# Destination one-hots compared in 16 bits by VectorE and spread to fp32 by ScalarE

## The chip, the cores and the metric

The kernel runs on one core of a Trainium2 chip. Its time is the device time of that core, in microseconds, from runs of the whole program. One core has five engines that each run their own list of instructions in order: TensorE (PE; its weight loads are shown as PEld), VectorE (DVE), ScalarE (ACT), GpSimd (POOL) and SyncE (SP), whose list here only issues DMAs. They wait for each other through semaphores.

## The reference

Four graph layers on 3125 nodes with 128 features and 103,125 edges sorted by destination, each followed by a residual and a layer norm. What matters here is the third layer's sum of edge attributes (64 features) per destination, and the number of edges per node, which the other layers use:

```python
agg = jax.ops.segment_sum(edge_attr, col, num_segments=x.shape[0])
h = jnp.concatenate([x, agg, u[batch]], axis=1)
...
x = _layernorm(x + _L0_gnn_ref(x, W1, b1, W2, b2, edge_index), axis=-1)
x = _layernorm(x + _L1_gnn_ref(x, src, dst, ...), axis=-1)
x = _layernorm(x + _L2_gnn_ref(x, edge_index, edge_attr_64, u, batch0, ...), axis=-1)
x = _layernorm(x + _L3_gnn_ref(x, src, dst, ...), axis=-1)
```

## The kernel before

The first 222 us build two things from the edge list; the rest (the four layers proper) multiplies node features with a matrix of edge counts and is not touched by the change.

**The loop.** It runs over 32 groups g. A group holds 20 blocks of 5 destinations, for which the counts between sources and destinations are made, and 4 edge blocks of 25 destinations (`EB` = 4, `EW` = 25), for which the attributes are summed. The last group has a quarter of both. No scheduler sets the order: each engine's list is written out, and semaphores tie them.

- VectorE makes three one-hots per group: `oh_lo` (L1119, 5000 elements of bf16) and `oh_key` (L1124, 4000 elements), both laid in pairs of 16-bit values and used for the counts, and `oh_dst` (L1157): for every edge slot of the 4 edge blocks, 32 per partition (`TE` = 8 each), 25 values that say which destination it has. `oh_dst` is fp32 and lies in `rowb`; it is made from int32 destinations `dst_e` with one scalar_tensor_tensor (add, then is_equal with `iota_w`). In the first groups VectorE also makes lists of edges (`make_lists`), and in group 5 some checks.
- TensorE waits for `oh_lo` and `oh_key` of a group, makes its 5 units of 4 blocks (L1740, L1744) in 5 banks, then waits for `dst_hot` and for the attributes (`ea_ready`) and makes the attribute products: per edge block 8 fp32 products with `oh_dst` as weights (L1756) and 8 with the upper halves of the same fp32 one-hots, read as bf16, for the number of edges (L1760). Then it folds the sums of the group before (`fold_quads`, L1701), and in groups 17 to 30 it does one step for x (transposes, L1715, or x times W, L1725).
- ScalarE copies each unit from its bank to `counts` (L802, five per group), keeps the attribute sums (`keep_apart`, L769, after the products of this group), keeps the folded ones (`keep_edges`, L775, after the fold of the group before), issues two of the loads of destinations (`odd_list`, L761), and in groups 17 to 30 keeps the x step (L783 or L789). In the first groups it also keeps lists (`keep_lists`, L746, L748).
- SP issues one attribute load of 256 KB per edge block (L583), up to 8 blocks ahead, each after the products of the block 8 before; for every second block a load of destinations (L575); and along blocks 36 to 60 the loads of x (L589).

Semaphores of this part: `dst_ready` (destinations landed), `dst_hot` (`oh_dst` made), `ea_made` (an edge block's products done), `apart_kept`, `apart_made` and `ea_kept` (the three steps behind it), `unit_made` and `unit_kept`.

Of the kernel before, what the change touches and what calls it, by code (L numbers as in the profile page):

```python
# [46 lines left out]
EW = 25  # L47
# [29 lines left out]
def gnn_program(nc, x, src, dst, edge_attr, p, out):  # L77

    with ExitStack() as ctx:
# [91 lines left out]
        def carve(n):  # L171
# [3 lines left out]
        iota_l = carve(128).bitcast(BF16).rearrange("p (l j) -> p l j", j=2)  # L175
        iota_w = wl1[:, 400:400 + EB * TE * EW].rearrange("p (j w) -> p j w", w=EW)
        dst_e = carve(RD * TE).bitcast(I32).rearrange("p (r j) -> p r j", r=RD)
        starts_i = carve(NE + 1)[0:1, :].bitcast(I32)
        key_base = carve(NQ)
# [64 lines left out]
            "bias_split ea_twice fold_made fold_kept masks_made l2_b1 l2_b2 bu_made flag_part flag_made "  # L244
            "deg_turned xw_made xw_kept apart_made apart_kept g_table_made g_key_made g_hot g_used g_kept o_table_made o_key_made o_hot o_used o_kept deg_again g_idx_seen before_made before_summed next_in sqrt_made"
        ).split()}
# [400 lines left out]
        def _(pool):  # L647
# [6 lines left out]
            for m in (ident, ident_bf, ident_h):  # L654
# [8 lines left out]
                           allow_small_or_imprecise_dtypes=True)  # L663
            nc.gpsimd.iota(iota_w, pattern=[[EW, EB], [0, TE], [1, EW]], base=0, channel_multiplier=0,
                           allow_small_or_imprecise_dtypes=True)
            for a, n in ((0, NQ - 1), (NQ - 1, 1)):
# [48 lines left out]
        def _(act):  # L715
# [40 lines left out]
            def odd_list(e):  # L756
# [4 lines left out]
                act.dma_start(dst_e[:, e % RD, :], dst[bass.ds(first, ECAP)].rearrange("(p j) -> p j", j=TE)).then_inc(dst_ready[e // EB % 3], 16)  # L761

            def keep_apart(g):

                ne = len(edge_blocks(g))
                act.wait_ge(s["ea_made"], EB * g + ne)
                if g >= 2:
                    act.wait_ge(s["apart_made"], g - 1)
                nc.scalar.activation(apart[:, g % 2, 0:ne, :], bank[5 + g % 2][:, 0:ne * (DE + 1)].rearrange("p (k f) -> p k f", k=ne), ACT.Copy).then_inc(s["apart_kept"], 1)  # L769
# [22 lines left out]
            for e in range(1, RD, 2):  # L792
                odd_list(e)
            keep_lists(0)
            act.wait_ge(s["pad_made"], 1)
            for g in range(NGP):
                for u, (ug, i, n) in enumerate(UNITS):
                    if ug != g:
                        continue
                    act.wait_ge(s["unit_made"], u + 1)  # L800
                    d0 = (g * GB + i) * BW
                    nc.scalar.activation(counts[:, :, d0:d0 + n * BW],  # L802
                                         bank[u % UB][:LO, 0:n * BK].rearrange("p (d h) -> p h d", h=HI), ACT.Copy).then_inc(s["unit_kept"], 1)
                if 1 <= g + 1 < NQ:
                    keep_lists(g + 1)
# [220 lines left out]
        def _(dve):  # L1026
# [86 lines left out]
            for g in range(NGP):  # L1113
# [38 lines left out]
                ne = len(es)  # L1152
                dve.wait_ge(dst_ready[g % 3], 16 * sum(len(edge_blocks(i)) for i in range(g % 3, g + 1, 3)))
                if g >= 2:
                    dve.wait_ge(s["ea_made"], EB * (g - 1))
                r0 = es[0] % RD
                nc.vector.scalar_tensor_tensor(oh_dst[r][:, 0:ne * TE, :],  # L1157
                                               dst_e[:, r0:r0 + ne, :].rearrange("p e (j a) -> p (e j) a", a=1).to_broadcast([128, ne * TE, EW]), -float(EB * g * EW),
                                               iota_w[:, 0:ne * TE, :],
                                               ALU.add, ALU.is_equal).then_inc(s["dst_hot"], 1)  # L1160

# [975 lines left out]
```

## Time and profile before

| | us |
|---|---|
| median of 3 runs | 818.76 (818.02 to 819.24) |
| the profiled execution | 820.66 |
| its span, first to last instruction | 818.6 |
| busy in the span: TensorE | 716.1 |
| VectorE | 585.3 |
| ScalarE | 330.6 |
| the loop over the groups | 26 to 222 |

The page gives for each engine its busy time in the span; these are averages over stages with different limits, so the loop has to be read by itself, through busy times of stretches, the order in time of one engine, and the chain of waits. The profiled execution is a single one, 1.9 us longer than the median; 2.1 us of it lie outside the span. Instructions of one engine overlap a little: the next may start before the last has ended, so what an instruction costs its queue is the distance from start to start.

### The profile page before, as it was taken

To read this page: it belongs to the slowest core of one execution; us is meant where nothing else is said; L and a number is where in the kernel's file an instruction comes from. 1 tells how busy PE (TensorE), PEld (TensorE's weight loads), DVE (VectorE), ACT (ScalarE), POOL (GpSimd) and SP (SyncE) were. 2 spreads that over 40 slices of the span, in tenths; PEclk is the share of its full clock that TensorE was granted. 3 is DMA by queue.
4 is the path that set the end of the run, shared out by engine and by line. 5 is a ranking of instruction groups with operands and counts; after the bars stand their busy time and mean duration, and the time that the engine had idled before them with its cause. 6 is when DMAs were issued, how large, how long until landed. Compare 5 with 4: busy or idle time off the path is not lost.

```text
span 818.6 us, 18498 instructions
## 1 busy us (share of the span) xinstructions
PE 716.1 (87%) x7630; PEld 640.1 (78%) x7630; DVE 585.3 (71%) x885; ACT 330.6 (40%) x594; POOL 25.5 (3%) x44
## 2 busy tenths in 40 slices
PE   4476776888889998999989998779969999999994
PEld 2366766888889998899979995445549998799994
DVE  6999999999776678778777764667576454145554
ACT  0365554666653224322462232363333332332243
POOL 4700000000000000000000000000000000000000
PEclk9777989999879999999999999989989999999998
DMA  4455677767530000000000000000000000000001
GB/s 104 136 136 160 180 213 204 190 186 211 143 84 1 1 1 1 1 1 1 2 22 1 1 1 2 0 14 0 1 26 1 0 0 1 1 1 1 1 26 54
DMA packets 48320, 43.14 MB, mean 53 GB/s; under 512 B 25989, under 2 KB 30759, under 8 KB 48167
## 3 DMA queue, kind: packets, MB, share of 16 engines
q1 hardware_dynamic: 35660, 39.80, 17.3%
q10 hardware_dynamic: 11932, 0.81, 1.0%
q8 instruction: 63, 1.03, 0.5%
q0 software_dynamic: 640, 1.29, 0.5%
q14 instruction: 25, 0.20, 0.1%
HBM read 39.08 MB, written 2.00 MB: 50 GB/s over the span
## 4 chain that ended last, share of the span: by engine, by line
PE 66%; DVE 16%; SPq 8%; issue 4%; ACT 2%; DMA 2%; DVEq 0%; ACTq 0%
PE bank L1823 21%; PE bank L1824 21%; SPq L583 3%; SPq L575 3%; PE bank L2024 2%; SPq L580 2%; DVE early L1119 2%; PE bank L1740 2%; PE bank L1756 2%; PE bank L2032 2%; PE bank L1885 1%; DVE early L1124 1%; PE bank L2075 1%; PE bank L2076 1%; PE bank L1744 1%
## 5 line engine op out<-in xcount | busy, mean ns | idle before, releaser
L1823 PE MATMUL bank<-stage,f_hi 125*128 125x392 f32 x1000 | 348.6, 349 | 2.5 <-issue 2.3
L1824 PE MATMUL bank<-stage,f_lo 125*128 125x392 f32 x1000 | 342.3, 342 | 0.0
L1202 DVE CAST stage<-counts 125x2352 fp32r<-125x2352 uint8 x120 | 164.4, 1380 | 80.8 <-PE bank L1824 80.7
L846 ACT ACTIVATE stage<-counts 125x1568 fp32r<-125x1568 uint8 x80 | 108.1, 1351 | 227.2 <-PE bank L1824 224.8
L1823 PEld LDWEIGHTS bank<-stage,f_hi 125*128 125x128 f32 x1000 | 189.8, 190 | 4.1 <-issue 2.4
L1824 PEld LDWEIGHTS bank<-stage,f_lo 125*128 125x128 f32 x1000 | 189.7, 190 | 0.6
L1740 PE MATMUL bank<-early 128*128 128x125 bf16 x625 | 76.8, 241 | 31.3 <-issue 24.0
L802 ACT ACTIVATE counts<-bank 125x500 uint8<-125x500 f32 (+1 forms) x157 | 81.2, 595 | 43.0 <-PE bank L1744 39.8
L1740 PEld LDWEIGHTS bank<-early 128*128 128x128 bf16 x625 | 68.2, 111 | 33.6 <-issue 33.6
L1119 DVE TENSOR_TENSOR early<-tmp 128x5000 bf16<-128x5000 bf16 (+1 forms) x32 | 86.4, 2700 | 1.4 <-PE bank L1744 1.4
L1744 PE MATMUL bank<-early 128*128 128x75 bf16 x625 | 76.2, 218 | 2.3 <-issue 2.1
L1124 DVE TENSOR_TENSOR early<-tmp,early 128x4000 bf16<-128x4000 bf16 (+1 forms) x32 | 70.2, 2193 | 0.0
L1744 PEld LDWEIGHTS bank<-early 128*128 128x128 bf16 x625 | 67.4, 109 | 2.4 <-issue 2.3
L1357 DVE SCALAR_TENSOR_TENSOR tmp<-bank,counts 125x2000 uint8<-125x2000 uint8 (+7 forms) x32 | 45.5, 1423 | 1.4
L1756 PE MATMUL bank<-wb,rowb 128*32 128x64 f32 x1520 | 36.2, 239 | 11.4 <-DMA wb<-in_edge_attr 6.0
L1756 PEld LDWEIGHTS bank<-wb,rowb 128*32 128x32 f32 x1520 | 29.3, 120 | 15.6 <-issue 13.3
L1157 DVE SCALAR_TENSOR_TENSOR rowb<-tmp,wl 128x800 f32<-128x800 int32 (+1 forms) x32 | 31.1, 971 | 0.1
L1885 PEld LDWEIGHTS bank<-ident,wa 128*125 128x125 f32 x100 | 17.8, 234 | 16.6 <-issue 7.2
L1760 PE MATMUL bank<-wb,rowb 128*32 128x1 bf16 x1000 | 28.8, 168 | 0.8 <-issue 0.8
L1885 PE MATMUL bank<-ident,wa 128*125 128x128 f32 x100 | 19.4, 321 | 11.1 <-ACT wb L878 6.4
L1280 DVE TENSOR_TENSOR f_lo<-bank,f_hi 125x512 fp32r<-125x512 f32 (+1 forms) x14 | 8.4, 631 | 26.7 <-ACT f_hi L860 26.7
L1249 DVE TENSOR_TENSOR wa<-bank,rowb 128x392 f32<-128x392 f32 x16 | 9.1, 567 | 24.0 <-PE bank L1824 23.8
(248 smaller groups left out, 848.1 us busy)
## 6 DMA issues: line engine op xcount, KB each, us to landing
wb<-in_edge_attr SPq DMA_DIRECT2D x95, 256.0 KB, 3.2
rowb<-in_edge_attr SPq DMA_DIRECT2D x30, 256.0 KB, 3.3
wa<-in_x SPq DMA_DIRECT2D x12, 125.0 KB
out<-wl SPq DMA_DIRECT2D x6, 250.0 KB
tmp<-in_dst SPq DMA_DIRECT2D x63, 4.0 KB, 2.9
tmp<-in_dst ACTq DMA_DIRECT2D x62, 4.0 KB, 2.8
eaT<-eaT SPq DMA_DIRECT2D x1, 784.0 KB, 6.0
wb<-in_L_gnn_w_ih SPq DMA_DIRECT2D x1, 384.0 KB, 3.4
```

The lines of the kernel that those rows point to most:

```text
L802: nc.scalar.activation(counts[:, :, d0:d0 + n * BW], bank[u % UB][:LO, 0:n * BK].rearrange("p (d h) -> p h d", h=HI), ACT.Copy).then_inc(s ...
L846: nc.scalar.activation(set_buffer(u, m), counts[:, SETS[u][0]:sum(SETS[u]), chunk(c)], ACT.Copy).then_inc(s["set_a_ready"], 1)
L1119: nc.vector.tensor_tensor(oh_lo[r][:, 0:n, 0:LO, :], iota_l.rearrange("p (a l) j -> p a l j", a=1)[:, :, 0:LO, :].to_broadcast([128, n, LO ...
L1124: hot = nc.vector.tensor_tensor(oh_key[r][:, 0:half, :, :, :].rearrange("p b m k j -> p (b m) k j"), iota_l.rearrange("p (a l) j -> p a l ...
L1202: nc.vector.tensor_copy(set_buffer(u, m), counts[:, SETS[u][0]:sum(SETS[u]), chunk(pair * 2 + off)]).then_inc(s["set_d_ready"], 1)
L1357: nc.vector.scalar_tensor_tensor(junk.rearrange("p (g l q) -> p g l q", g=n, q=2), turned, 0.0, own, ALU.add, ALU.not_equal, accum_out=unl ...
L1740: mm(bank[u % UB][:, b * BK:(b + 1) * BK], oh_lo[r][:, i + b, :, 0], keys[:, 0:BK], start=True, stop=False)
L1744: last = mm(bank[u % UB][:, b * BK + 2 * HI:(b + 1) * BK], oh_lo[r][:, i + b, :, 1], keys[:, BK:NK * HI], start=False, stop=True)
L1756: mm(bank[5 + r][quad:quad + 32, k * (DE + 1):k * (DE + 1) + DE], oh_dst_row[r][:, at:at + 32], ea_in[e % RE][:, j, :], start=(j < 4), sto ...
L1823: mm(bank[h][:, 0:CH], f_hi[:, first + k, :], rhs[:, k, :], start=(first + k == 0), stop=False)
L1824: last = mm(bank[h][:, 0:CH], f_lo[:, first + k, :], rhs[:, k, :], start=False, stop=(first + k == HI - 1))
L1885: last = nc.tensor.transpose(bank[NORM_BANK[i][k]][:LO, h * D:(h + 1) * D], norm_columns(i, k, h), ident[:, :])
```

## The change

Where `oh_dst` was made by one instruction of VectorE in 32 bits, it is now made in three steps. ScalarE shortens the destinations of a group to bf16, minus the group's first destination (`shorten`, 32 elements per partition, one group ahead, behind the units of the group before). VectorE compares them in 16 bits in pairs (tensor_tensor, is_equal, 800 elements) with numbers that `iota_l` already holds, into `oh_short`. ScalarE spreads these bf16 one-hots to fp32 in their old place (`spread_bits`), behind the second of the five unit copies of the same group. Two semaphores are new: `dst_short` and `dst_bits`. `dst_hot` now comes from ScalarE. `iota_w` and its iota on GpSimd are gone.

```diff
-        iota_w = wl1[:, 400:400 + EB * TE * EW].rearrange("p (j w) -> p j w", w=EW)
+        oh_short = [wl1[:, 400 + r * nh // 2:400 + (r + 1) * nh // 2].bitcast(BF16).rearrange("p (j w t) -> p j w t", w=EW, t=2) for r in range(2)]
+        dst_short = carve(EB * TE).bitcast(BF16).rearrange("p (r j t) -> p r j t", r=2, t=2)
...
-            nc.gpsimd.iota(iota_w, pattern=[[EW, EB], [0, TE], [1, EW]], base=0, channel_multiplier=0,
-                           allow_small_or_imprecise_dtypes=True)
...
+            def shorten(g):
+
+                es = edge_blocks(g)
+                act.wait_ge(dst_ready[g % 3], 16 * sum(len(edge_blocks(i)) for i in range(g % 3, g + 1, 3)))
+                if g >= 2:
+                    act.wait_ge(s["dst_bits"], g - 1)
+                n, r0 = len(es), es[0] % RD
+                nc.scalar.activation(dst_short[:, g % 2, 0:n * TE // 2, :].rearrange("p j t -> p (j t)"), dst_e[:, r0:r0 + n, :].rearrange("p r j -> p (r j)"),
+                                     ACT.Copy, bias=-float(EB * g * EW)).then_inc(s["dst_short"], 1)
+
+            def spread_bits(g):
+
+                n = len(edge_blocks(g)) * TE
+                act.wait_ge(s["dst_bits"], g + 1)
+                if g >= 2:
+                    act.wait_ge(s["ea_made"], EB * (g - 1))
+                nc.scalar.activation(oh_dst[g % 2][:, 0:n, :].rearrange("p (j t) w -> p j t w", t=2), oh_short[g % 2][:, 0:n // 2, :, :].rearrange("p j w t -> p j t w"),
+                                     ACT.Copy).then_inc(s["dst_hot"], 1)
...
             keep_lists(0)
+            shorten(0)
...
                                          bank[u % UB][:LO, 0:n * BK].rearrange("p (d h) -> p h d", h=HI), ACT.Copy).then_inc(s["unit_kept"], 1)
+                    if i == 4:
+                        spread_bits(g)
+                if g + 1 < NGP:
+                    shorten(g + 1)
...
-                dve.wait_ge(dst_ready[g % 3], 16 * sum(len(edge_blocks(i)) for i in range(g % 3, g + 1, 3)))
+                dve.wait_ge(s["dst_short"], g + 1)
                 if g >= 2:
-                    dve.wait_ge(s["ea_made"], EB * (g - 1))
-                r0 = es[0] % RD
-                nc.vector.scalar_tensor_tensor(oh_dst[r][:, 0:ne * TE, :],
-                                               dst_e[:, r0:r0 + ne, :].rearrange("p e (j a) -> p (e j) a", a=1).to_broadcast([128, ne * TE, EW]), -float(EB * g * EW),
-                                               iota_w[:, 0:ne * TE, :],
-                                               ALU.add, ALU.is_equal).then_inc(s["dst_hot"], 1)
+                    dve.wait_ge(s["dst_hot"], g - 1)
+                shape = [128, ne, TE // 2, EW, 2]
+                half = ne * TE // 2
+                nc.vector.tensor_tensor(oh_short[r][:, 0:half, :, :].rearrange("p (k j) w t -> p k j w t", k=ne),
+                                        iota_l[:, 0:ne * EW, :].rearrange("p (k a w) t -> p k a w t", k=ne, a=1).to_broadcast(shape),
+                                        dst_short[:, r, 0:half, :].rearrange("p (k j) (a t) -> p k j a t", k=ne, a=1).to_broadcast(shape),
+                                        ALU.is_equal).then_inc(s["dst_bits"], 1)
```

On ScalarE, in a group with an x step (such as 27), this stood before: the five unit copies (L802), the two keeps, two list loads and the keep of an x step. `counts`, `wl` (the sums), `eaT` (the folded ones) and `xT` are what is written; `bank` is PSUM.

```order
L802 ACTIVATE counts<-bank 125x25x20 [waits unit_made] x5
L769 ACTIVATE wl<-bank 128x260 [waits apart_made,ea_made]
L775 ACTIVATE eaT<-bank 65x100 [waits apart_made]
L760 TENSOR_LOAD tmp
L761 REGISTER_ALU
L761 DMA tmp<-in_dst 128x8
L760 TENSOR_LOAD tmp
L761 REGISTER_ALU
L761 DMA tmp<-in_dst 128x8
L783 ACTIVATE xT<-bank 128x500 [waits xt_made]
```

And this stands there now, up to the keep of the x step, which follows as before (line numbers are those of the changed kernel):

```order
L821 ACTIVATE counts<-bank 125x25x20 [waits unit_made] x2
L778 ACTIVATE rowb<-wl 128x800 [waits ea_made,dst_bits]
L821 ACTIVATE counts<-bank 125x25x20 [waits unit_made] x3
L769 ACTIVATE tmp<-tmp 128x32 [waits dst_bits,dst_ready0]
L787 ACTIVATE wl<-bank 128x260 [waits apart_made,ea_made]
L793 ACTIVATE eaT<-bank 65x100 [waits apart_made]
L759 TENSOR_LOAD tmp
L760 REGISTER_ALU
L760 DMA tmp<-in_dst 128x8
L759 TENSOR_LOAD tmp
L760 REGISTER_ALU
L760 DMA tmp<-in_dst 128x8
```

The spread (L778) has come behind the second copy, and the shortening (L769) between the last copy and the keeps; nothing else moved.

On VectorE a group of three instructions, and the two after it, before:

```order
L1119 TENSOR_TENSOR early<-tmp 128x20x250 [waits unit_made,list_kept]
L1124 TENSOR_TENSOR early<-tmp,early 128x4000
L1157 SCALAR_TENSOR_TENSOR rowb<-tmp,wl 128x800 [waits ea_made,dst_ready1]
L1119 TENSOR_TENSOR early<-tmp 128x20x250 [waits unit_made,list_kept]
L1124 TENSOR_TENSOR early<-tmp,early 128x4000
```

And now:

```order
L1142 TENSOR_TENSOR early<-tmp 128x20x250 [waits unit_made,list_kept]
L1147 TENSOR_TENSOR early<-tmp,early 128x4000
L1181 TENSOR_TENSOR wl<-tmp 128x800 [waits dst_hot,dst_short]
L1142 TENSOR_TENSOR early<-tmp 128x20x250 [waits unit_made,list_kept]
L1147 TENSOR_TENSOR early<-tmp,early 128x4000
```

The compare keeps its place; it waits for two semaphores of ScalarE instead of a DMA and TensorE, and writes `wl` (where `oh_short` lies) instead of `rowb`.

## Rows read from the trace of the kernel before

**Rows 1.** Busy us (instructions) of each engine in two stretches; granted clock, DMA share, GB/s.

```profile
core 0: us, PE busy (x) PEld busy (x) DVE busy (x) ACT busy (x) POOL busy (x), PEclk, DMA share, GB/s
...
95.00:133.00 38.00, 28.07 (x894) 26.68 (x895) 38.00 (x21) 19.26 (x43) 0.00 (x0) 0.91 0.72 203
...
148.00:222.00 74.00, 66.42 (x2101) 62.96 (x2098) 70.74 (x40) 49.42 (x113) 0.00 (x0) 0.95 0.69 185
```

**Rows 2.** Order in time, VectorE, one group: start us, duration us, instruction.

```profile
199.34 0.99 DVE L1157 SCALAR_TENSOR_TENSOR rowb<-tmp,wl 128x800 f32<-128x800 int32 x1
200.24 2.76 DVE L1119 TENSOR_TENSOR early<-tmp 128x5000 bf16<-128x5000 bf16 x1
202.91 2.24 DVE L1124 TENSOR_TENSOR early<-tmp,early 128x4000 bf16<-128x4000 bf16 x1
205.07 0.99 DVE L1157 SCALAR_TENSOR_TENSOR rowb<-tmp,wl 128x800 f32<-128x800 int32 x1
```

**Rows 3.** The chain of waits, 176 to 200 us, shares by line.

```profile
by line: SPq L583 23.4%; SPq L575 21.7%; SPq L580 14.6%; issue 12.8%; DMA wb<-in_edge_attr 12.6%; PE bank L1756 5.6%; PE bank L1725 4.2%; PE bank L1701 2.4%; PE bank L1740 1.6%; PE bank L1760 0.8%; PE bank L1744 0.5%
```

**Rows 4.** Order in time, SP's queue: x loads, then block 72, then block 121.

```profile
124.46 0.36 SPq L589 DMA_DIRECT2D wa<-in_x  x1
...
127.55 0.35 SPq L589 DMA_DIRECT2D wa<-in_x  x1
...
143.29 0.63 SPq L583 DMA_DIRECT2D wb<-in_edge_attr  x1
...
212.03 3.04 SPq L583 DMA_DIRECT2D wb<-in_edge_attr  x4
```

**Rows 5.** Order in time, ScalarE: first copies of groups 17 and 28.

```profile
146.96 2.50 ACT L802 ACTIVATE counts<-bank 125x500 uint8<-125x500 f32 x5 [1.41 <-PE bank L1744]
...
206.41 2.98 ACT L802 ACTIVATE counts<-bank 125x500 uint8<-125x500 f32 x5 [0.49 <-PE bank L1744]
```

**Rows 6.** Order in time, ScalarE: a group with hardly a wait.

```profile
185.13 2.50 ACT L802 ACTIVATE counts<-bank 125x500 uint8<-125x500 f32 x5
187.47 0.44 ACT L769 ACTIVATE wl<-bank 128x260 f32<-128x260 f32 x1
...
189.87 2.50 ACT L802 ACTIVATE counts<-bank 125x500 uint8<-125x500 f32 x5
```

**Rows 7.** Order in time, VectorE: a small 16-bit compare and its successor.

```profile
218.83 0.32 DVE L1129 TENSOR_TENSOR tmp<-tmp,wl 128x300 bf16<-128x300 bf16 x1
219.06 0.37 DVE L1157 SCALAR_TENSOR_TENSOR rowb<-tmp,wl 128x200 f32<-128x200 int32 x1
```

**Rows 8.** Groups of ScalarE's instructions by shape: busy us, mean ns, idle before.

```profile
L846 ACT ACTIVATE stage<-counts 125x1176 fp32r<-125x1176 uint8 x40 | 47.5, 1187 | 149.5 <-PE bank L1824 149.5
...
L825 ACT ACTIVATE f_hi<-wa 125x512 fp32r<-125x512 f32 x6 | 3.2, 627 | 0.0
...
L746 ACT ACTIVATE tmp<-bank 128x252 bf16<-128x252 bf16 x5 | 1.9, 377 | 12.7 <-PE bank L1693 12.7
```

**Rows 9.** Order in time, all engines: group 27's steps, and group 28's products.

```profile
200.42 2.50 ACT L802 ACTIVATE counts<-bank 125x500 uint8<-125x500 f32 x5
...
201.77 0.43 PE L1756 MATMUL bank<-wb,rowb 128*32 128x64 f32 x16
...
203.17 0.39 ACT L769 ACTIVATE wl<-bank 128x260 f32<-128x260 f32 x1 [0.25 <-PE bank L1760]
...
203.69 0.25 ACT L775 ACTIVATE eaT<-bank 65x100 f32<-65x100 f32 x1
...
205.34 0.59 ACT L783 ACTIVATE xT<-bank 128x500 f32<-128x500 f32 x1 [1.40 <-issue]
...
208.70 0.65 PE L1756 MATMUL bank<-wb,rowb 128*32 128x64 f32 x16
...
211.21 0.25 ACT L775 ACTIVATE eaT<-bank 65x100 f32<-65x100 f32 x1
```

**Rows 10.** Order in time, ScalarE and its DMA issues (ACTq).

```profile
155.19 0.34 ACTq L761 DMA_DIRECT2D tmp<-in_dst  x1
155.55 0.45 ACT L769 ACTIVATE wl<-bank 128x260 f32<-128x260 f32 x1
```

More of the change, by code:

```diff
@@ L244, in gnn_program @@
             "bias_split ea_twice fold_made fold_kept masks_made l2_b1 l2_b2 bu_made flag_part flag_made "
-            "deg_turned xw_made xw_kept apart_made apart_kept g_table_made g_key_made g_hot g_used g_kept o_table_made o_key_made o_hot o_used o_kept deg_again g_idx_seen before_made before_summed next_in sqrt_made"
+            "deg_turned xw_made xw_kept apart_made apart_kept g_table_made g_key_made g_hot g_used g_kept o_table_made o_key_made o_hot o_used o_kept deg_again g_idx_seen before_made before_summed next_in sqrt_made dst_short dst_bits"
         ).split()}
```

## The prediction

> **What bounds the kernel now.** The change touches only the loop over the 32 groups, 26 to 222 us, so I took the busy times of two stretches of it: in 38 us VectorE works 38.0, TensorE 28.1, ScalarE 19.3; in the last 74 us they work 70.7, 66.4 and 49.4 [rows 1]. VectorE is full. Its order in time says why: one group is three instructions, starting at 199.34, 200.24 and 202.91, and the next group's first starts at 205.07. A group takes 5.73 us, of which the compare of destinations (L1157) holds 0.90 [rows 2].
>
> That is not yet the bound of the loop's end. The chain of waits from 176 to 200 us lies on SP's queue, 23.4, 21.7 and 14.6% in its three lines, then on the landing of a load [rows 3]. SP issues two attribute loads and one list of destinations per two edge blocks. Block 72 was issued at 143.29 and block 121 at 212.03: 68.7 us for 49 blocks, 5.6 us per group of four. Between 88 and 130 us it also issues the 13 loads of x, and then two blocks take 3.1 us (124.46 to 127.55), 6.2 us per group [rows 4]. So three things lie close together: VectorE 5.73, SP 5.6, and 6.2 in groups 9 to 15, where the products run late behind the loads. Later the kernel catches up: ScalarE begins group 17 at 146.96 and group 28 at 206.41, 11 groups in 59.45 us, 5.40 each [rows 5].
>
> **ScalarE's cycle before.** In a group that waits for almost nothing ScalarE starts five copies at 185.13, the keep of the sums at 187.47 (2.34 later) and the next group's copies at 189.87: 4.74 us, one step of x included [rows 6]. That is 1 us below VectorE's cycle. This room is what lets the loop catch up.
>
> **The change, part by part.** (1) *VectorE's compare.* The old one, 800 elements of 32 bits, holds 0.90 us [rows 2]. The new one has 800 elements of 16 bits laid in pairs, like L1119 and L1124, which hold 2.67 us for 5000 and 2.16 for 4000 elements: 0.51 us per 1000. L1129, 300 elements of the same kind, holds 0.23 us (218.83 to 219.06) [rows 2, 7]. So 800 elements hold 0.23 + 0.5 x 0.51 = 0.49 us (0.52 by the line through the large two), and VectorE's cycle falls by 0.41 to 5.32 us; over 31 groups that is 12.7 us if nothing else counted. Bounds: 0.49, and 0.90 if pairs bring nothing here.
>
> The Trainium skill, "VectorE: DVE Perf Modes", section What auto-detection actually checks, states that the engine takes two elements per cycle if every tensor is of 16 bits with step one. The broadcast operand repeats one pair over 25 places, so by a strict reading the compare would stay at 0.90 us; but L1124 repeats its pairs in the same way, and its 2.24 us for 4000 elements show that this is enough [rows 2].
>
> (2) *ScalarE gets two instructions per group.* The spread reads 800 16-bit elements in SBUF with a step of two and writes 800 of fp32. Nearest rows, from SBUF to SBUF: 512 elements in 0.627 us, 1176 in 1.187; between them 800 take 0.87. L746, 252 elements of 16 bits read with a stride (from PSUM), takes 0.377, no more than its size explains [rows 8]. From start to start it is some 0.11 less than the duration (a copy of 0.6 us holds 0.48), so 0.76. The shortening of 32 elements I take at 0.15, below what the 252 of L746 hold. ScalarE's queue grows by 0.91: 4.74 becomes 5.65 even where nothing is waited for. Bounds of the spread: 0.80, and 1.1 if a strided 16-bit source in SBUF is slower.
>
> (3) *A new order between the engines.* Before, the attribute products (L1756) waited for VectorE, long done by then. Now they wait for ScalarE's spread, behind its second copy, and ScalarE's keeps wait for those products. One group, counted from ScalarE's first copy: two copies, 0.96; spread, done at 1.83; to TensorE 0.05, 1.88; from the start of the products to the keep that waits for the fold (201.77 to 203.69) 1.92, so 3.80; from that keep over two list loads to the next instruction (203.69 to 205.34) 1.65, so 5.45; the keep of an x step 0.49, so 5.94 [rows 9]. Beside it lies ScalarE's own work, five copies, spread and shortening, 2.40 + 0.76 + 0.15 = 3.31; the products end at 1.88 + 1.40 (201.77 to 203.17) = 3.28. So ScalarE's cycle is **5.45 us without an x step and 5.94 with one**. Behind its waiting keeps stand the list loads and all copies of the next group; TensorE waits with the next products. VectorE waits for shortened lists that are there 3.3 us into the group before, in time.
>
> (4) GpSimd loses one iota before the loop, beside other waits: nothing. SP's queue has no new instruction. TensorE has none either.
>
> **Sum.** Until SP reaches its x loads (groups 0 to 8) VectorE's lists and ScalarE's 5.45 leave 0.3 us or less per group of gain, some 1.5 to 2 us. In groups 9 to 15 SP's 6.2 exceeds 5.45, and nothing changes. I keep -1.0 at group 17. Groups 17 to 27 all have an x step: 11 x 5.94 = 65.3 instead of 59.45, +5.9. About one of them meets the lower clock (the first 16 products take 0.65 instead of 0.43 us, and products and fold 2.5 instead of 1.9 us [rows 9]): +0.6. Groups 28 to 30 have no list loads, so TensorE and ScalarE alternate alone: the products began 2.29 us after the first copy in group 28 (206.41, 208.70) and 1.35 in the usual one (200.42, 201.77), now 1.88: -0.4 + 0.5 + 0.5 = +0.6 [rows 5, 9]. In the last group, of 5 blocks, the products came right behind the units; now two copies and a spread of 200 elements stand ahead, 0.7 + 0.4 = +1.1. Together -1.0 + 5.9 + 0.6 + 0.6 + 1.1 = **+7.2 us**, and nothing changes behind the loop. The profiled execution took 820.66 us (a span of 818.6 and 2.1 around it), so the same view would show 827.8; from the median of 818.76, 1.9 lower, it is **825.9 us**.
>
> **Rivals.** *Faster, with SP as the bound (0.15).* ScalarE may issue its list loads while copies still run: one was issued at 155.19, ahead of the keep at 155.55 that precedes it in the program [rows 10]. If the keeps' waits are over when the queue comes to them, up to 1.2 of the 1.65 us is hidden, the cycle is 4.7 us, below VectorE's 5.32 and SP's 5.6, and SP sets the end. It gains only what it gains before its x loads, at most 9 x 0.41 = 3.7, less the 1.1 of the last group: 816 us. Against it: in (3) both waits end late, at 3.28 and 3.80, and where a keep waited the load stood behind it (203.69, then 205.34) [rows 9]. The Trainium skill, "Advanced Engine Details and Errata", section Engine Queue Depths, gives ScalarE eight places, which would allow it to run ahead so; no row shows it past a wait that is still open.
>
> *Nothing measurable (0.13).* If the second keep comes 0.26 behind the first, the cycle is 5.68, and with a spread of 0.80, 5.61: 11 x 0.21 = +2.3, the last groups +1.7, less up to 3.7 at the start: 819 us.
>
> *Slower by more (0.2).* TensorE stands still ahead of each group's products, and five further groups may run at 1.2 GHz, +0.6 each, 3 us; a spread of 1.1 us adds 0.23 to 14 groups, 3.2 us: 832 us.
>
> *The change doesn't make the compare faster.* At 0.90 us VectorE stays at 5.73, below 5.94; only the gain at the start is lost: 827 us, within the forecast. So the sign does not hang on VectorE but on whether ScalarE's cycle exceeds 5.4 us, the pace of groups 17 to 27.
>
> **Numbers.** The forecast as worked out 0.52 (822 to 830), the rivals 0.15, 0.13 and 0.2. The range of 815.5 to 834 takes in all of these but their far ends. 0.2%, 1.6 us, is about what a measurement tells from no change: faster 0.15, same 0.13, slower 0.72.
>
> **What would show it.** In the profile of the changed kernel: the compare (L1181) at 0.57 us, 0.49 to the next start; the spread (L778) at 0.87; idle time of VectorE ahead of its one-hots; ScalarE's first copies 5.9 us apart from group 17 on; TensorE idle ahead of the attribute products, released by ScalarE; the loop's end at about 229 us instead of 222. I am wrong if the groups with x run at 5.5 us or less, if list loads stand ahead of the keeps, or if the spread takes over 1 us.

## The result, and the profile after

| | before | changed |
|---|---|---|
| median, us | 819.00 (818.02 to 819.37, 4 runs) | 828.43 (825.24 to 831.70, 4 runs) |
| the profiled execution, us | 820.66 | 831.70 |
| its span, us | 818.6 | 829.7 |

The changed kernel takes 1.0109 times as long, with an interval of 1.0081 to 1.0137: slower, by 9.4 us between the medians. The forecast was 825.9 us. The changed kernel's profiled execution is the slowest of its four, 3.3 us over their median. In it the loop over the groups ends at 234.60 us (VectorE's first instruction behind it, L1188) against 222.06 for the same instruction before, 12.5 us later, while the whole span is only 11.1 us longer. So the loss lies in the loop.

The chain that ended last, over the whole span, by engine, changed:

```profile
PE 68%; DVE 14%; ACT 7%; issue 4%; SPq 3%; ACTq 2%; DMA 2%; DVEq 0%
```

ScalarE and its DMA issues, 2% and 0% of it before, are 7% and 2% now; SP fell from 8% to 3%.

VectorE in order of time (start us, duration us, instruction), first where nothing holds it and then where it is held; square brackets give the idle time before an instruction and who ended it:

```profile
58.46 2.76 DVE L1142 TENSOR_TENSOR early<-tmp 128x5000 bf16<-128x5000 bf16 x1
...
63.28 0.57 DVE L1181 TENSOR_TENSOR wl<-tmp 128x800 bf16<-128x800 bf16 x1
63.77 2.76 DVE L1142 TENSOR_TENSOR early<-tmp 128x5000 bf16<-128x5000 bf16 x1
...
202.94 0.57 DVE L1181 TENSOR_TENSOR wl<-tmp 128x800 bf16<-128x800 bf16 x1 [2.48 <-ACT tmp L769]
...
208.90 0.58 DVE L1181 TENSOR_TENSOR wl<-tmp 128x800 bf16<-128x800 bf16 x1 [0.56 <-ACT tmp L769]
```

The compare holds VectorE for 0.49 us (63.28 to 63.77) instead of 0.90 [rows 2], and a group takes 5.31 us (58.46 to 63.77) instead of 5.73. The edit does what it says. But VectorE now stands idle ahead of the compare, released by ScalarE's shortening. The same two stretches as in [rows 1], busy us of each engine, granted clock, DMA share, GB/s:

```profile
95.00:133.00 38.00, 26.92 (x864) 25.85 (x864) 32.33 (x19) 23.60 (x55) 0.00 (x0) 0.87 0.75 204
148.00:222.00 74.00, 58.85 (x1756) 56.61 (x1757) 60.60 (x35) 51.44 (x117) 0.00 (x0) 0.89 0.65 170
```

No engine is full any longer. VectorE's busy time in the last 74 us fell from 70.7 to 60.6, TensorE's from 66.4 to 58.9, and ScalarE, which has more to do per group, works 51.4 instead of 49.4. Everybody waits, and the waits from 26 to 232 us say for whom (us in total, times, longest):

```profile
PE bank L1780 <- ACT rowb L778: 30.8, 25, 2.4
...
DVE wl L1181 <- ACT tmp L769: 24.7, 18, 3.7
```

TensorE waits 31 us for the spread, VectorE 25 us for the shortening. In the kernel before VectorE never stood still between 95 and 133 us (38.00 of 38 us busy [rows 1]), though TensorE worked 28.07 there; now it works 32.33 of 38. The new instructions by shape, same stretch (busy us, mean ns, idle before):

```profile
L778 ACT ACTIVATE rowb<-wl 128x800 f32<-128x800 bf16 x31 | 27.2, 877 | 5.2 <-DVE wl L1181 5.2
L1181 DVE TENSOR_TENSOR wl<-tmp 128x800 bf16<-128x800 bf16 x31 | 17.8, 575 | 23.1 <-ACT tmp L769 22.6
L769 ACT ACTIVATE tmp<-tmp 128x32 bf16<-128x32 int32 x30 | 7.8, 259 | 0.0
```

And one turn of the ring, group 26 with its x step, ScalarE, its DMA issues (ACTq) and TensorE's first products:

```profile
205.50 1.06 ACT L821 ACTIVATE counts<-bank 125x500 uint8<-125x500 f32 x2
...
206.44 0.89 ACT L778 ACTIVATE rowb<-wl 128x800 f32<-128x800 bf16 x1
...
207.37 0.43 PE L1780 MATMUL bank<-wb,rowb 128*32 128x64 f32 x16 [1.68 <-ACT rowb L778]
...
209.29 0.25 ACT L793 ACTIVATE eaT<-bank 65x100 f32<-65x100 f32 x1
...
209.74 1.17 ACTq L760 DMA_DIRECT2D tmp<-in_dst  x2
...
210.96 0.60 ACT L807 ACTIVATE wa<-bank 125x512 f32<-125x512 f32 x1 [1.42 <-PE bank L1749]
...
211.45 1.06 ACT L821 ACTIVATE counts<-bank 125x500 uint8<-125x500 f32 x2
```

From the group's first copy: products at 1.87, keep of the fold at 3.79, list loads issued at 4.24, keep of the x step at 5.46, next group at 5.95. While the list loads are issued ScalarE does nothing and TensorE, which has long made the next units, waits for its spread. Groups without an x step do the same without the last keep, 5.46 us from first copy to first copy:

```profile
88.59 1.07 ACT L821 ACTIVATE counts<-bank 125x500 uint8<-125x500 f32 x2 [1.40 <-PE bank L1768]
...
94.05 1.06 ACT L821 ACTIVATE counts<-bank 125x500 uint8<-125x500 f32 x2 [1.41 <-PE bank L1768]
```

### The profile page after: what moved, and what is told of

The parts are those of the page before. It is cut to its first block, busy times and chain, and to the rows that moved or that the text cites. A ratio compares the mean times of both kernels' runs of the same rounds, so it can differ in the third digit from the quotient of the medians.

```text
span 829.7 us, 18621 instructions
## 1 busy us (share of the span) xinstructions
PE 718.9 (87%) x7630; PEld 643.0 (77%) x7630; DVE 574.3 (69%) x885; ACT 355.9 (43%) x658; POOL 23.7 (3%) x43
## 4 chain that ended last, share of the span: by engine, by line
PE 68%; DVE 14%; ACT 7%; issue 4%; SPq 3%; ACTq 2%; DMA 2%; DVEq 0%
PE bank L1847 21%; PE bank L1848 21%; PE bank L1780 4%; ACT rowb L778 2%; PE bank L2048 2%; PE bank L1725 2%; ACT counts L821 2%; PE bank L2056 2%; PE bank L1764 2%; ACTq L760 1%; PE bank L1909 1%; PE bank L2099 1%; PE bank L2100 1%; PE bank L1860 1%; DVE early L1142 1%
## 5 line engine op out<-in xcount | busy, mean ns | idle before, releaser
L1181 DVE TENSOR_TENSOR wl<-tmp 128x800 bf16<-128x800 bf16 (+1 forms) x32 | 18.1, 565 | 25.2 <-ACT tmp L769 24.7
L778 ACT ACTIVATE rowb<-wl 128x800 f32<-128x800 bf16 (+1 forms) x32 | 27.6, 861 | 5.2 <-DVE wl L1181 5.2
L1909 PE MATMUL bank<-ident,wa 128*125 128x128 f32 x100 | 19.4, 321 | 11.1 <-ACT wb L901 6.4
```

What stands on the lines that cost most here:

```text
L1909: last = nc.tensor.transpose(bank[NORM_BANK[i][k]][:LO, h * D:(h + 1) * D], norm_columns(i, k, h), ident[:, :])
```

## The experiments

The theory: the loop is held by a **ring**, ScalarE's copies, its spread, TensorE's products, ScalarE's keeps, the list loads behind them, and the next group's copies. The rivals: the added load on ScalarE by itself (0.91 us per group), the compare, and SP's queue. Twelve kernels were run, in three rounds of four, each round beside the kernel before (medians 819.3, 819.7 and 819.8 us); the ratios are to that. The changed kernel itself ran in none of these rounds, so a difference to its 828.4 us is good to about 1 us.

### Load without the ring

The kernel before, with ScalarE doing the same two copies idly, nobody waiting for them. Nothing of the computation is left out.

```diff
+                    if i == 4 and g < NGP - 1:
                         ...                  (waits only for its own last idle copy)
+                        nc.scalar.activation(idle_out[:, 0:800]..., idle_in[:, 0:800]..., ACT.Copy).then_inc(s["idle_made"], 1)
+                if g < NGP - 1:
+                    nc.scalar.activation(idle_out[:, 800:832], idle_in[:, 0:32], ACT.Copy).then_inc(s["idle_made"], 1)
```

> The kernel before, with two idle instructions added to ScalarE's list where the change puts its own: a spread of 800 elements behind the second copy and one of 32 behind the fifth, into memory that nobody reads; VectorE and TensorE wait for none of them. Ring theory: ScalarE's cycle is 5.65 us with an x step, no more than VectorE's 5.73, and the only loss is that groups 17 to 27 can no longer catch up at 5.40: 0 to +3 us, ratio 1.000 to 1.004. Load theory: as slow as the changed kernel or slower, since VectorE has no relief, ratio 1.011 or more.

Measured: 818.97 us, 0.9996 (0.9984 to 1.0008). Two first copies of this kernel (its line L805), and a list load between them:

```profile
190.69 1.06 ACT L805 ACTIVATE counts<-bank 125x500 uint8<-125x500 f32 x2
...
193.88 0.36 ACTq L761 DMA_DIRECT2D tmp<-in_dst  x1
...
195.58 1.06 ACT L805 ACTIVATE counts<-bank 125x500 uint8<-125x500 f32 x2
```

With the whole added work ScalarE still turns in 4.89 us, since the first list load is issued (193.88) while its last small copy runs. The load costs nothing here, where nobody waits for the two copies; load as a cause falls.

### The compare twice

The changed kernel, VectorE making each compare once more into unused space:

```diff
+                if g < NGP - 1:
                     ...                      (waits only for its own last idle compare)
+                    nc.vector.tensor_tensor(idle[:, 0:half, :, :]..., iota_l..., dst_short..., ALU.is_equal).then_inc(s["idle_made"], 1)
```

> The changed kernel with VectorE's 16-bit compare made twice in each group (the first into memory that nobody reads), so that VectorE's cycle is back at about 5.8 us, what it was before the change. Ring theory: 5.8 is still below the 5.94 of the x groups, so only the first groups lose: +1 to +3 us, ratio 1.012 to 1.015. Rival (VectorE still sets the pace and its relief of 0.4 us per group counts): +0.5 us in each of 31 groups, +15 us, ratio 1.03.

Measured: 829.1 us, 1.0124 (1.0097 to 1.0151), against 1.0109 (1.0081 to 1.0137) for the changed kernel: the intervals overlap, the medians differ by 0.7 us, where the ring theory had said 1 to 3 us. So 0.49 us more per group on VectorE, 15 us over the loop, is absorbed almost whole, and the 0.41 us that the compare gained was not on the path either.

### The spread one copy sooner

The changed kernel with the spread behind the first unit copy of the group instead of the second.

```diff
-                    if i == 4:
+                    if i == 0:
                         spread_bits(g)
```

> The changed kernel with the spread one copy sooner (behind the first of ScalarE's five unit copies, not the second). Ring theory (ScalarE's cycle of 5.45 and 5.94 us is a ring: copies, spread, attribute products, keep, list loads): the ring falls to 4.97 and 5.46, below ScalarE's own work of 5.71 with an x step and below VectorE's 5.32 without one, so the x groups take 5.7 instead of 5.94: 2.5 us for 11 groups and some 1 us in the last ones, about 824.5 us, ratio to before 1.006 to 1.007. Rival, load theory (only the 0.9 us of added ScalarE work counts, wherever it stands): no change against the changed kernel, ratio 1.011.

Measured: 819.29 us, 1.0004 (0.9981 to 1.0027). The direction was right and the size was not: 9 us came back where 3 to 4 were expected. The group with an x step turns in 5.45 us instead of 5.94:

```profile
191.35 0.58 ACT L821 ACTIVATE counts<-bank 125x500 uint8<-125x500 f32 x1
...
194.56 0.43 ACT L787 ACTIVATE wl<-bank 128x260 f32<-128x260 f32 x1
194.83 0.28 ACT L793 ACTIVATE eaT<-bank 65x100 f32<-65x100 f32 x1
195.10 1.16 ACTq L760 DMA_DIRECT2D tmp<-in_dst  x2
...
196.80 0.58 ACT L821 ACTIVATE counts<-bank 125x500 uint8<-125x500 f32 x1
```

Neither keep waits here (0.27 us apart, as ScalarE's own pace has it), and the list loads start 0.27 behind the second instead of 0.45. ScalarE's own work had been taken for a second limit close by, at 5.71; it is at 5.45. Eleven groups at 5.45 instead of 5.94 are 5.4 us. The clock is a further part: this kernel's trace shows a granted clock of 1.00 from 148 to 200 us, the changed kernel's 0.86, where two groups that met the lower level cost 3.4 us (see the terms of the sum below). Together that is about what came; whether the spread's new place kept the clock up was not tried by itself.

### The list loads ahead of the keeps

The changed kernel with ScalarE's two list loads issued before its keeps.

```diff
+                for e in range(EB * g + RD + 1, min(EB * g + RD + EB, NE), 2):
+                    odd_list(e)
                 keep_apart(g)
                 if g:
                     keep_edges(g - 1)
-                for e in range(EB * g + RD + 1, min(EB * g + RD + EB, NE), 2):
-                    odd_list(e)
```

> The changed kernel with ScalarE's two list loads issued ahead of the two keeps instead of behind them (their slots were read one group before, so the data allow it). Ring theory: the 1.65 us from the second keep to the next instruction falls to about 0.3, the issue of the loads lies beside the copies that still run, and the ring is 4.1 us without and 4.6 with an x step. VectorE's 5.32 and SP's pace of 5.6 are next: groups 17 to 27 at 5.4 to 5.6 us, the loop's end 7 to 11 us earlier than in the changed kernel, 817 to 821 us, ratio 0.998 to 1.003. Rival, load theory (ScalarE's work is the same, in another order): ratio 1.011, unchanged.

Measured: 816.23 us, 0.9963 (0.9950 to 0.9976): 12 us less than the changed kernel and now faster than before, by moving two small DMA issues past a wait. ScalarE in this kernel:

```profile
187.87 1.06 ACT L821 ACTIVATE counts<-bank 125x500 uint8<-125x500 f32 x2
...
189.82 0.34 ACTq L760 DMA_DIRECT2D tmp<-in_dst  x1
190.03 1.09 ACT L821 ACTIVATE counts<-bank 125x500 uint8<-125x500 f32 x2
190.63 0.34 ACTq L760 DMA_DIRECT2D tmp<-in_dst  x1
...
192.61 1.07 ACT L821 ACTIVATE counts<-bank 125x500 uint8<-125x500 f32 x2
```

The issues lie beside running copies, and the group turns in 4.74 us. That is a group that nothing holds; over groups 17 to 27 it is 5.52 us on average (144.03 to 204.80), for other limits than the ring bind now. The control is the same edit in the kernel before, where no ring exists (with one more wait, for `dst_hot` of the group, ahead of the list loads):

> The kernel before with the one edit that helped the changed kernel: ScalarE issues its two list loads of a group (odd_list) ahead of the keeps instead of behind them (they now wait for dst_hot of the group first). ScalarE's cycle in a group with an x step was 4.74 us with hardly a wait; VectorE's is 5.73. Ring theory: in the kernel before nobody waits for the keeps, so 1 us more of room for ScalarE is worth nothing: 0.998 to 1.001 of the time before. Rival (the edit is good by itself, because the lists land earlier or because SP's queue profits, and its gain in the changed kernel says nothing about a ring): the gain of the changed kernel, 828.4 to 816.2, would show here too, 0.985 to 0.99.

Measured: 819.02 us, 0.9990 (0.9979 to 1.0000). So the edit is worth nothing measurable by itself, and its 12 us belong to the ring.

### One idle copy, in the ring and beside it

The changed kernel with one more copy of ScalarE, 400 elements of 16 bits to fp32. First ahead of the spread:

```diff
                     if i == 4:
                         ...                  (not in the last group; waits only for its own last idle copy)
+                        nc.scalar.activation(early[:, 11624:12024]..., iota_l...[:, :, 0:200].to_broadcast([128, 2, 200]), ACT.Copy).then_inc(s["idle_made"], 1)
                         spread_bits(g)
```

> The changed kernel with one idle copy of ScalarE more per group, 400 16-bit elements spread to fp32, right ahead of the spread, about 0.5 us long and 0.41 from start to start. Ring theory: it lies in the ring, so every group that the ring binds is 0.41 longer, some 22 of 32: +9 us, a ratio of 1.019 to 1.024. Rival, ScalarE's own work (3.31 us and the rest) is not the limit and half of it is absorbed: 1.011 to 1.016.

Then behind the shortening, ahead of the keeps:

```diff
                 if g + 1 < NGP:
                     shorten(g + 1)
                 ...                          (not in the last group; waits only for its own last idle copy)
+                nc.scalar.activation(early[:, 11624:12024]..., iota_l...[:, :, 0:200].to_broadcast([128, 2, 200]), ACT.Copy).then_inc(s["idle_made"], 1)
```

> The same idle copy in another place: behind the shortening, ahead of the keeps, where ScalarE waits for the products and the fold. ScalarE's own work up to there is then 3.31 + 0.41 = 3.72 us against products that end at 3.28 and a fold at 3.80: the second keep comes at 3.72 + 0.29 = 4.0 instead of 3.8, so +0.2 us per group, half of what the copy costs ahead of the spread: +4 us, a ratio of 1.013 to 1.018. Rival, load theory: place doesn't matter, and both idle kernels cost the same. Rival, the waits hide it: 1.011.

Measured: 838.72 us, 1.0247 (1.0215 to 1.0279), ahead of the spread; 828.85 us, 1.0116 (1.0094 to 1.0137), behind the shortening, which is the changed kernel's own time. The same instruction costs 10 us in one place, a little more than the 9 expected, and nothing in the other, so place decides, not load. The first of the two:

```profile
199.83 1.06 ACT L822 ACTIVATE counts<-bank 125x500 uint8<-125x500 f32 x2
200.76 0.55 ACT L828 ACTIVATE early<-tmp 128x400 f32<-128x400 bf16 x1
201.19 0.89 ACT L778 ACTIVATE rowb<-wl 128x800 f32<-128x800 bf16 x1
...
206.19 1.06 ACT L822 ACTIVATE counts<-bank 125x500 uint8<-125x500 f32 x2
```

It holds 0.43 us (200.76 to 201.19), and the cycle is 6.36 instead of 5.94: 0.42 more. The second:

```profile
199.49 1.06 ACT L822 ACTIVATE counts<-bank 125x500 uint8<-125x500 f32 x2
...
202.70 0.58 ACT L831 ACTIVATE early<-tmp 128x400 f32<-128x400 bf16 x1
...
203.39 0.27 ACT L793 ACTIVATE eaT<-bank 65x100 f32<-65x100 f32 x1
203.72 1.18 ACTq L760 DMA_DIRECT2D tmp<-in_dst  x2
...
205.44 1.06 ACT L822 ACTIVATE counts<-bank 125x500 uint8<-125x500 f32 x2
```

The cycle is 5.95, unchanged, where 0.2 more was expected: of what was said beforehand, the rival that the waits hide it came true. The second keep does come 0.1 later (3.90 behind the first copy instead of 3.79), but the loads behind it start 4.23 behind the first copy, as they did (4.24).

### The fold ahead of the products

The changed kernel, TensorE folding the group before ahead of its wait for the spread:

```diff
+                if g:
+                    fold_quads(g - 1)
                 ...                          (the waits and the attribute products of g)
-                if g:
-                    fold_quads(g - 1)
```

> The changed kernel, with one step of TensorE's order moved: it folds the sums of the group before (fold_quads of g - 1) ahead of the attribute products of g, not behind them. The fold then runs while TensorE would wait for the spread, and the second keep of ScalarE no longer waits for it behind the products. Ring theory: the ring is then two copies 0.96, spread to 1.83, TensorE 1.88, products 1.40, the first keep at 3.28 with 0.39 busy, the second at about 3.65 instead of 3.80, then 1.65 to the keep of the x step: 5.3 without an x step and 5.8 with one, 0.15 less per group, 11 to 25 groups: 2 to 4 us less than the changed kernel, a ratio of 1.006 to 1.009. Rival 1 (the fold takes from TensorE what it gives, since TensorE works at its own bound there): 1.011, no change. Rival 2 (the fold now waits for keep_apart of the group before, and pauses TensorE ahead of the products): over 1.013. TensorE's order is what changes, so the keep of the fold should wait less by the profile, under 0.3 us per group.

Measured: 819.47 us, 0.9994 (0.9977 to 1.0010). Again the sign was right, and 9 us came instead of 2 to 4. One turn, with an x step:

```profile
199.02 1.06 ACT L821 ACTIVATE counts<-bank 125x500 uint8<-125x500 f32 x2
...
199.13 0.62 PE L1725 MATMUL bank<-wl 128*65 128x25 f32 x8
...
200.89 0.43 PE L1782 MATMUL bank<-wb,rowb 128*32 128x64 f32 x16 [1.14 <-ACT rowb L778]
...
202.58 0.24 ACT L793 ACTIVATE eaT<-bank 65x100 f32<-65x100 f32 x1
202.74 1.17 ACTq L760 DMA_DIRECT2D tmp<-in_dst  x2
...
204.45 1.06 ACT L821 ACTIVATE counts<-bank 125x500 uint8<-125x500 f32 x2
```

The products start 1.87 behind the first copy as ever, but the fold (199.13) now lies in TensorE's idle time. The keep behind it comes at 3.56 instead of 3.79, and the loads at 3.72 instead of 4.24: 0.5 off the ring (5.43 instead of 5.94), more than half of it the shorter distance from a keep that has not waited to the issue behind it (0.16 instead of 0.45). Over groups 17 to 27 that makes 5.6 us; where the rest of the 9 comes from is open. The granted clock, 0.93 from 148 to 200 us instead of 0.86, may be part of it.

### The loads of x from another queue

GpSimd issues the 13 loads of x, at the same edge blocks, and SP doesn't:

```diff
             (SP, at edge blocks 36 to 60)
-                    sp.dma_start(wa[:LO, h * D:(h + n) * D], x[...]).then_inc(s["x_in"], 16)
             (GpSimd)
+            for h in range(0, HI, 2):
+                pool.wait_ge(s["ea_made"], X_FROM + h - RE + 1)
+                pool.dma_start(wa[:LO, h * D:(h + n) * D], x[...]).then_inc(s["x_in"], 16)
```

First in the changed kernel with the list loads ahead of the keeps:

> The changed kernel with the list loads ahead of the keeps (816.2 us) and, on top, the 13 loads of x issued by GpSimd instead of SP, each after the same edge block as before. In groups 9 to 15 SP's queue sets the pace in all kernels so far, 6.2 us per group with x loads among its issues against 5.6 without. Theory that the issues are the bound there: 7 groups by 0.4 to 0.6 us, 3 to 4 us less: 812 to 813.5, a ratio of 0.992 to 0.994. Rival, the landing of the attribute loads is the bound (256 KB each, at the bandwidth that the DMA engines have beside the x loads): the same bytes take the same time and nothing changes, 0.995 to 0.998. The first copies of groups 9 to 16 tell it: 5.3 to 5.6 us apart by the first, over 6 by the rival.

Measured: 809.21 us, 0.9871 (0.9848 to 0.9894): faster than both kernels and 7 us less than with the list loads ahead alone, twice the 3 to 4 us expected. VectorE in what were the slow groups:

```profile
107.26 2.75 DVE L1142 TENSOR_TENSOR early<-tmp 128x5000 bf16<-128x5000 bf16 x1
...
112.57 2.75 DVE L1142 TENSOR_TENSOR early<-tmp 128x5000 bf16<-128x5000 bf16 x1
```

It runs at its own 5.31 us per group, and is busy 38.00 of the 38 us from 95 to 133 and 51.81 of the 52 from 148 to 200. Here the faster compare is paid out, though SP, at 5.39 us per group from block 72 to 121 (131.94 to 198.01), has hardly any room left. Then in the kernel before, and in the changed kernel without the other edit:

> The kernel before with the one edit that took the changed kernel (list loads ahead) from 816.2 to 809.2 us: the 13 loads of x issued by GpSimd instead of SP. VectorE's cycle here is 5.73 us per group, SP's with the x loads 6.2. Theory (in groups 9 to 15 SP binds, elsewhere VectorE): 7 groups by 0.4 to 0.5, but the loop also caught up afterwards, groups 17 to 27 at 5.4 each, and this debt is then gone: VectorE at 5.73 from group 4 (65.82) to 31 ends at 221 instead of 221.4 in the profile, so 0.998 to 1.000. Rival (the issues of SP are the bound of the whole loop and VectorE isn't): about 7 us less, as in the changed kernel, 0.99. If the first holds, the faster compare is needed for the gain of 10 us: 0.41 us by 24 groups.

> The changed kernel with the x loads issued by GpSimd alone; the list loads stay behind the keeps. Ring theory: groups 5 to 15 and 28 to 30 at ScalarE's 5.45 us, groups 17 to 27 at 5.94; g8 88.6, g17 about 138 instead of 146.5, g28 about 204 instead of 217.4 with its stalls, so 8 to 12 us less than the changed kernel, 817 to 820 us, a ratio of 0.998 to 1.002, and 8 us or more above the kernel that has the list loads ahead as well (809.2). Rival (SP's queue was what cost the changed kernel its time, and the ring mattered little): 809 to 812, 0.988 to 0.992.

Measured: before with it 819.05 us, 0.9991 (0.9981 to 1.0001), nothing; changed with it 821.96 us, 1.0035 (1.0018 to 1.0051), 2 us above what the ring theory expected at most, 6.5 us less than the changed kernel and 13 more than with the list loads ahead as well. In the kernel before, VectorE at 5.73 us is the bound of the whole loop (with x on GpSimd it is busy 38.00 of 38 and 52.00 of 52 us in the same two stretches), and the x loads only shift work inside it. In the changed kernel ScalarE's ring and, in groups 9 to 15, SP each hold the loop. Why late loads cost the changed kernel 6.5 to 7 us and the kernel before nothing can be read from VectorE. Before, its compare needs nothing that ScalarE computes, and it works on (38.00 of 38 us from 95 to 133), so the others catch up behind it. Now its compare waits for a shortening that stands in ScalarE's list behind the copies, and what holds ScalarE holds VectorE: 33.28 of 38 us even with the list loads ahead, and 38.00 again with the x loads on GpSimd too. No kernel was run that removes this wait alone. With both out of the way VectorE binds again, and the difference between the two kernels that have the x loads on GpSimd, 819.05 and 809.21, is 9.8 us, which would be the 0.41 us of the compare over some 24 groups.

### All together

The last kernel with the spread sooner and the fold ahead as well:

> The changed kernel with four edits: the spread behind the first copy instead of the second, the list loads ahead of the keeps, the x loads issued by GpSimd, and the fold of the group before ahead of the products. If ScalarE's ring is all that kept the faster compare from paying, VectorE with 5.32 us per group and SP with 5.6 are the bound now; the ring itself is 4.76 to 5.3 with the loads ahead, less 0.4 for the earlier spread. Expected 811 to 814 us, a ratio of 0.990 to 0.994. If the parts hide one another, it is the best of them, 816 us, 0.996. If SP's issues set the end of the loop by themselves (49 blocks in 68.7 us before), the gain ends at groups 0 to 15 and it is 814 to 816 us.

Measured: 809.56 us, 0.9871 (0.9845 to 0.9896), no better than without the two, and below what either theory expected. The ring is shorter than VectorE's cycle in both, so shortening it further buys nothing. That SP would stop the gain at 814 us was wrong, since its pace was taken too slow: blocks 72 to 121 are issued at 5.42 us per group here (134.79 to 201.13), not 5.6. But SP is close: from 95 to 205 us it waits for no product in this kernel, it only issues, and VectorE with 5.31 us per group is busy 50.54 of the 52 us from 148 to 200. Which of the two would hold a kernel that is faster still, these runs do not separate.

## Why the prediction was right

The sign and the mechanism are as forecast: 9.4 us lost between the medians where 7.2 were said, through the ring. That the time came so near is in part luck, for two terms were off in opposite directions, as the parts below show.

**The compare** (0.49 us to the next start, VectorE's cycle 5.32): measured 0.49 and 5.31.

**ScalarE's two instructions**: the spread 0.877 us long with 0.76 to the next start (206.44 to 207.20), as said. The shortening's duration is 0.26 us; taken for 0.15 of the queue, it is 0.17 to 0.18 to the keep behind it (188.29 to 188.46), and 0.12 where that next instruction waits for nothing (194.44 to 194.56 with the spread sooner).

**The ring**: 5.45 and 5.94 from first copy to first copy; measured 5.45 to 5.46 and 5.94 to 5.95, with products at 1.87 (1.88 said), the keep of the fold at 3.79 (3.80) and 1.67 from there over the list loads (1.65). This step carried the forecast, and the idle copy, the list loads and the fold confirm it from three sides. One part of it was wrong: VectorE was said to find its shortened lists in time. It waits for them 18 times, 24.7 us in all. In an undisturbed group that is 0.56 us (the row at 208.90), about what VectorE's cycle is shorter than the ring, and costs nothing; where ScalarE is held longer, VectorE loses work that it used to do ahead.

**ScalarE's own work, 5.65 beside it**: too high. With the spread sooner the cycle fell to 5.45 with all keeps on time. It only mattered for the expectation of that run.

**Groups 0 to 16, -1.0**: -0.5 in the profile (146.46 for [rows 5]'s 146.96), but -3.7 in the kernel with the idle copy behind the shortening (143.28), which takes the same time as the changed kernel. The term varies from execution to execution by more than its size. That SP holds groups 9 to 15 of the changed kernel was right: with the x loads elsewhere group 17 begins at 139.42, 7 us sooner. Of the kernel before it was misread. SP's pace there was not a bound of its own but made up for later, since that kernel did not gain from the same edit; VectorE's 5.73 was the bound on the whole.

**Groups 17 to 27, +5.9, and the slow clock, +0.6**: this is the term that was mis-sized. The first copies of groups 17 and 28 lie 70.93 us apart (146.46, 217.39) against 65.3 plus 0.6, and +11.5 instead of +6.5 against before. It is not this execution alone: in three other kernels with the same ring that stretch takes 69.71 (the compare twice), 70.62 (x loads on GpSimd) and 68.61 us (the idle copy behind). Half of the eleven groups take 5.94 or little more; the rest of the difference is in a few. A group at the lower clock was given 0.6 us more, for its products and its fold:

```profile
191.66 1.06 ACT L821 ACTIVATE counts<-bank 125x500 uint8<-125x500 f32 x2
...
196.79 0.25 ACT L793 ACTIVATE eaT<-bank 65x100 f32<-65x100 f32 x1 [0.55 <-PE bank L1725]
...
199.34 1.26 ACT L821 ACTIVATE counts<-bank 125x500 uint8<-125x500 f32 x2
```

The keep of the fold comes at 5.13 instead of 3.79 behind the first copy, and the next group at 7.68 instead of 5.94: 1.74 us for one group, and groups 17 and 24 are such, 3.4 us together. The 0.6 had been read from group 28 before (208.70 to 211.21 [rows 9]), which met the lower clock in part only. TensorE's products and fold in group 24, and then in that group before (the number before the DMA share is the granted clock):

```profile
193.50:196.80 3.30, 3.26 (x105) 3.25 (x106) 2.22 (x3) 1.93 (x6) 0.00 (x0) 0.50 0.56 158
...
208.70:211.20 2.50, 2.50 (x107) 2.48 (x106) 2.50 (x3) 0.99 (x3) 0.00 (x0) 0.73 0.42 72
```

0.50 is the lower level, 1.2 GHz, throughout. Products and fold take 3.26 us there (5.13 less 1.87) against 2.51 in the group the price came from and 1.92 at full clock. In two more, the issue of the list loads took 1.94 and 1.71 us instead of 1.17:

```profile
176.78 1.94 ACTq L760 DMA_DIRECT2D tmp<-in_dst  x2
...
189.42 1.71 ACTq L760 DMA_DIRECT2D tmp<-in_dst  x2
```

The kernel before had such issues too (two loads in 1.90 us at 177.62), but 1 us of room in ScalarE's cycle [rows 6]; the ring has none, and such a delay is added to the end. That the room is the difference was argued from these rows, not tried by itself; nor was what makes an issue take longer.

**Groups 28 to 31, +1.7**: +1.6 (the loop's end is 12.5 us later and group 28 began 11.0 later). **Behind the loop**, where nothing was to change, the span is 1.4 us shorter (11.1 more in all); no run looks into why, and executions of one kernel differ by as much.

**The rivals.** *SP as the bound, with list loads issued ahead* did not happen by itself: written behind a keep with an open wait, the loads came 0.45 us after that keep, in each of groups 17 to 27. Written ahead of the keeps they were issued under running copies (190.63 beside copies from 190.03 to 191.12), and the time was 816.2 us, where the rival had said 816. The Trainium skill, "Advanced Engine Details and Errata", section Engine Queue Depths, gives ScalarE eight places; by these rows they help as long as no instruction ahead has an open wait. *Nothing measurable* fell because the second keep does wait for the fold: it comes 0.51 us behind the first (208.78 and 209.29), where it comes 0.27 behind when nothing holds it. The first keep waits for some 0.05 us only; ScalarE's own work and the products end nearly together. *The compare not faster* fell by its 0.49 us. *Slower by more*, 832, named a share of what came: the granted clock from 148 to 222 us is 0.89 instead of 0.95, and two groups at the lower level cost 3.4 us; the spread was not slower than taken.

## What to carry to other kernels

When work moves from a full engine to one with room, don't add up busy times: draw the ring of who waits for whom, from start to start, and see what is queued behind its waits. Look also at what the old bottleneck now waits for: an engine that could run ahead through the others' delays may not be able to any more. A DMA issue behind a wait costs its whole time in such a ring, and ahead of the wait nothing; that was the difference between 9 us lost and 3 us gained. And a loop that has lost its last room adds up every small delay that it used to absorb, so its sum from undisturbed groups is a lower bound.

## What the runs showed of the hardware

- Two small DMA issues of ScalarE cost the kernel 12 us behind a keep that waits, and nothing ahead of it, where each takes 0.34 us beside running copies.
- From the start of a keep to the issue behind it there are 0.45 us where the keep had waited, 0.27 to 0.33 where it hadn't, and 0.16 in one kernel. Why they differ stays open.
- The spread reads 16-bit values with a step of two and writes fp32 in 877 ns for 800 elements. By the Trainium skill, "ScalarE: Activation LUTs", section What ACT_TABLE_LOAD costs, a copy takes 186 ns and 0.833 ns per element, 852 ns: the trace agrees within 3%, so the step costs next to nothing.
- VectorE's compare of 800 elements, with one operand that repeats a pair over 25 places and another that repeats 25 pairs over 4 rows, holds it for 0.49 us against 0.90 of the old 32-bit compare of as many elements, in line with the 0.51 us per 1000 elements of its other two one-hots.
